# A decoder layer on one core: the causal mask of the first attention by GpSimd's selects instead of TensorE's mask matmuls, with new instruction orders and PSUM banks for the loop

## The reference

```python
q, k, v = split(x @ qkv_w.T + qkv_b)            # 16 heads of 8
q, k = relu(q) + 1e-6, relu(k) + 1e-6
kv = cumsum(einsum('bhld,bhle->bhlde', k, v), axis=2)
num = einsum('bhld,bhlde->bhle', q, kv)          # token l sees the tokens up to l
den = maximum(einsum('bhld,bhld->bhl', q, cumsum(k, axis=2)), 1e-6)
x = layernorm(x + (num / den) @ out_w.T + out_b)
x = layernorm(x + window_attention(x, ctx, ctx) @ W_proj.T + b_proj)   # softmax, |distance| <= 64
x = layernorm(x + experts(x))    # top 1 of 8 experts, capacity 641, gelu, 512 hidden
```

## Time and profile before

| | |
|---|---|
| time, median of 3 runs | 474.26 us (473.88 to 474.88) |
| profiled execution, its own time | 473.45 us |
| span of its instructions | 471.7 us |
| mean granted clock | 0.962 |
| busy of the span: PE, PEld | 89%, 72% |
| DVE, ACT, POOL | 75%, 57%, 55% |
| stretch 100 to 300 us, busy of 200 us: PE | 196.3 us |
| the same, DVE, ACT, POOL | 175.7, 141.2, 123.2 us |

### The profile page before, as it was taken

The page is one execution under the profiler, slowest core; times in us unless marked ns, Lnnn a source line. Parts: engine busy times, 40 slices in busy tenths (PEclk is TensorE's granted clock), DMA queues, the critical chain, the costliest instruction groups (busy, mean ns, idle before and its releaser), DMA issues.

```text
span 471.7 us, 20960 instructions
## 1 busy us (share of the span) xinstructions
PE 422.2 (89%) x7850; PEld 337.8 (72%) x7850; DVE 351.5 (75%) x1670; ACT 268.1 (57%) x655; POOL 258.6 (55%) x374
## 2 busy tenths in 40 slices
PE   8889999999999999999999999998746699999950
PEld 7666777778777778777777777776535478887740
DVE  4466667888888888888888898887673277778750
ACT  4456667667767667777667777666532333345400
POOL 5422355655666655666655666654552046757753
PEclk9999999999999999999999999999975799999995
DMA  4800000110110110110100100000014223334000
GB/s 137 266 15 15 14 25 15 31 33 25 29 35 26 33 31 27 30 32 26 37 27 27 34 18 20 20 17 13 19 35 118 85 84 103 103 108 134 25 17 20
DMA packets 25719, 22.50 MB, mean 48 GB/s; under 512 B 3606, under 2 KB 21072, under 8 KB 25620
## 3 DMA queue, kind: packets, MB, share of 16 engines
q1 hardware_dynamic: 23284, 16.96, 12.3%
q0 software_dynamic: 2336, 4.20, 2.8%
HBM read 12.13 MB, written 9.58 MB: 46 GB/s over the span
## 4 chain that ended last, share of the span: by engine, by line
PE 65%; ACT 17%; issue 9%; DVE 3%; POOL 2%; DMA 2%; POOLq 0%; ACTq 0%; DVEq 0%; SPq 0%
PE banks L567 24%; PE banks L623 13%; PE banks L810 8%; ACT arena L836 7%; PE banks L575 7%; ACT arena L936 6%; ACT arena L835 4%; PE banks L560 4%; PE banks L787 3%; PE banks L635 1%; DMA expert_in<-x,sidx 1%; PE banks L536 1%; PE banks L720 1%; PE banks L807 1%; DMA EB<-expert_in 1%
## 5 line engine op out<-in xcount | busy, mean ns | idle before, releaser
L1080 DVE TENSOR_REDUCE mx<-banks 128x8 f32<-128x1024 f32 x64 | 77.9, 1219 | 21.1 <-PE banks L575 21.1
L440 POOL TENSOR_TENSOR rs<-ve,minus_half 128x1 f32<-128x1 f32 x32 | 18.3, 570 | 105.1 <-DVE ve L1047 105.1
L865 ACT ACTIVATE arena<-banks 128x1024 f32<-128x1024 f32 x64 | 62.0, 1021 | 15.0 <-PE banks L575 15.0
L835 ACT ACTIVATE arena<-banks,first_half 128x512 f32<-128x512 f32 x64 | 44.1, 689 | 46.4 <-PE banks L575 46.4
L623 PE MATMUL banks<-arena,V 128*32 128x128 f32 x2048 | 69.4, 276 | 0.1
L936 ACT ACTIVATE arena<-banks,b1T 128x321 f32<-128x321 f32 x64 | 33.8, 529 | 55.1 <-PE banks L787 54.4
L623 PEld LDWEIGHTS banks<-arena,V 128*32 128x32 f32 x2048 | 51.9, 109 | 9.6 <-issue 5.3
L502 POOL DMA_INDIRECT out_x<-ot,idx x40 | 40.5, 1012 | 24.5 <-DVE ot L1277 15.8
L471 POOL DMA_INDIRECT expert_in<-x,sidx x32 | 35.5, 1109 | 11.5 <-DVE x L1153 4.8
L567 PE MATMUL banks<-x1T,CE 32*128 32x128 f32 x1024 | 37.5, 282 | 4.5 <-ACT arena L836 0.6
L567 PE MATMUL banks<-QE,kT 32*128 32x128 f32 x1024 | 37.7, 282 | 3.4 <-DVE mx L1080 1.3
(11 more groups left out here) (175 smaller groups left out, 1025.4 us busy)
## 6 DMA issues: line engine op xcount, KB each, us to landing
w_sb<-in_L_ffn_W SPq DMA_DIRECT2D x16, 256.0 KB, 3.1
expert_in<-zeros SPq DMA_DIRECT2D x10, 266.5 KB, 3.6
EB<-expert_in SPq DMA_DIRECT2D x8, 325.0 KB, 4.2
X<-in_x SPq DMA_DIRECT2D x32, 64.0 KB, 2.0
C<-in_ctx SPq DMA_DIRECT2D x32, 64.0 KB, 2.7
out_x<-fb SPq DMA_DIRECT2D x32, 64.0 KB, 1.5
out_x<-ot,idx POOLq DMA_INDIRECT x40, 2.2
b2b<-in_L_ffn_b SPq DMA_DIRECT2D x1, 512.0 KB
```

The source lines that it names most:

```text
L835: nc.scalar.activation(to[:, :, :, 0:W2C], at_bank[:, :, :, 0:W2C], ACT.Relu, scale=first_half[:])
L865: nc.scalar.activation(P2[b % 2][:, 2 * half:2 * half + 2].rearrange("p j a t -> p j (a t)"), pair("s2t", half), ACT.Exp, scale=SCALE).the ...
L1080: v.tensor_reduce(mx[b % 2][:, 8 * half:8 * half + 8].rearrange("p (j a) -> p j a", a=NA), pair("s2", half).rearrange("p j (a t) -> p j a ...
```

## The change

The 8 mask matmuls of `op_s1` go, and so do ACT's half-width copies: ACT now copies each half of the scores with one 128x1024 instruction. A new pair of POOL operations, `op_sel0` and `op_sel1`, sets to zero, in place in A1, the pairs that are not allowed, and `op_pv1` waits for them (`causal`) instead of for ACT. The copies of xT and x1T move from DVE to ACT. The order lists of all four engines and the bank table are new. The lags of several entries change with the place in the list at which a pass is cut.

```diff
+JOBS = [("xT", 0, (5,)), ("x2T", 8, (3,)), ("y2T", 6, (2,)), ("pv2", 4, (4,)), ("s1", 1, (6, 7, 2, 3)),
...
+            def keep_earlier(b, half):
+
+                pool.wait_ge(s1_out[half], b + 1)
+                part = A1[b % 2][:, 2 * half:2 * half + 2].rearrange("p j a t -> p (j a) t")
+                g.affine_select(out=part, in_=part, compare_op=ALU.is_ge, fill=0.0, base=0,
+                                pattern=[[0, 2 * NA], [1, P]], channel_multiplier=-1).then_inc(causal[half], 1)
...
-                by_head("s1", lambda part, a: kT[b % 2][part, :], lambda part, a: QE[b % 2][part, a, :])
-                causal_masks(0)
-                causal_masks(1).then_inc(s1_full, 1)
+                mm = by_head("s1", lambda part, a: kT[b % 2][part, :], lambda part, a: QE[b % 2][part, a, :], alone=True)
+                mm.then_inc(s1_full, 1)
...
-                values("pv1", b, A1[b % 2], V1[b % 2], s1_out).then_inc(pv1_full, 1)
+                values("pv1", b, A1[b % 2], V1[b % 2], causal).then_inc(pv1_full, 1)
...
-                nc.scalar.activation(to[:, :, :, 0:W2C], at_bank[:, :, :, 0:W2C], ACT.Relu, scale=first_half[:])
-                nc.scalar.activation(to[:, :, :, W2C:P], at_bank[:, :, :, W2C:P], ACT.Relu).then_inc(s1_out[half], 1)
+                nc.scalar.activation(A1[b % 2][:, 2 * half:2 * half + 2].rearrange("p j a t -> p j (a t)"),
+                                     pair("s1", half), ACT.Relu).then_inc(s1_out[half], 1)
```

More of the change, by code:

```diff
@@ L257, in decoder @@
         s1_out = [sem(f"s1_out{k}") for k in range(2)]
+        causal = [sem(f"causal{k}") for k in range(2)]
         pv1_full, yx1_done, t1_full, y1_ready = sem("pv1_full"), sem("yx1_done"), sem("t1_full"), sem("y1_ready")
@@ L475, in _ @@
             for n in range(B + LAST):
-                at(op_x1b, n - 3)
[L477 to L483, removed]
+                at(op_pow2, n - 6)
+                at(op_v2, n - 2)
+                at(op_QE, n)
+                at(op_x2, n - 6)
+                at(op_xb, n)
+                at(op_x1b, n - 3)
+                at(op_sel0, n)
+                at(op_pow1, n - 1)
+                at(op_sel1, n)
+                at(op_x1, n - 1)
                 at(op_scatter, n - 8)
@@ L535, in busy @@
                 for _ in range(count):
-                    pe.matmul(banks[:, 7, 0:P], ident[:], ident[:], start=True, stop=True)
+                    pe.matmul(banks[:, 4, 0:P], ident[:], ident[:], start=True, stop=True)
             busy(6)
@@ L560, in turned, with by_head @@
                 return pe.transpose(bank(name)[0:rows, 0:P], src, ident[:])
-            def by_head(name, weights, moved, first=True):
+            def by_head(name, weights, moved, first=True, alone=False):
                 for a in range(NA):
@@ L566, in by_head @@
                         part = slice(VW * j, VW * (j + 1))
-                        pe.matmul(banks[:, used, a * P:(a + 1) * P], weights(part, a), moved(part, a),
-                                  start=first and a == 0, stop=False, tile_position=(VW * j, 0))
+                        mm = pe.matmul(banks[:, used, a * P:(a + 1) * P], weights(part, a), moved(part, a),
+                                       start=alone or first and a == 0, stop=alone, tile_position=(VW * j, 0))
+                return mm
             lo, hi = slice(0, W2C), slice(W2C, P)
@@ L576, in masked @@
                                  tile_position=(at_rows.start, rows.start))
[L578 to L583, removed]
             def window_masks(name, half):
@@ L732, in _ @@
                     pe.wait_ge(setup_done, 1)
+                at(op_x2T, n - 8)
+                at(op_y2T, n - 6)
+                at(op_pv2, n - 4)
+                at(op_s1, n - 1)
+                at(op_y1T, n - 2)
+                at(op_lg, n - 8)
                 at(op_o2, n - 6)
@@ L828, in copied, with op_xTe @@
                 nc.scalar.copy(dst[:], bank(name)[:, 0:P]).then_inc(done, 1)
+            def op_xTe(b):
+                act.wait_ge(xT_full, b + 1)
+                wait(act, qkv_full, b - 1)
+                copied(xT[b % 2], "xT", xT_done)
             def op_s1e(b, half):
@@ L847, in op_yx1, with op_x1Te @@
                 nc.scalar.copy(yx1[:].rearrange("p j t -> p (j t)"), bank("pv1")[:, 0:2 * P]).then_inc(yx1_done, 1)
+            def op_x1Te(b):
+                act.wait_ge(x1T_full, b + 1)
+                wait(act, s2t_full, b - 1)
+                copied(x1T[b % 2], "x1T", x1T_done)
             def op_CE(b):
@@ L915, in _ @@
             for n in range(B + LAST):
+                at(op_x2Te, n - 8)
+                at(op_y2Te, n - 6)
+                at(op_yx2, n - 4)
+                at(op_xTe, n)
                 at(op_s1e0, n - 1)
@@ L1199, in _ @@
                     other_constants()
+                at(op_rec2, n - 4)
+                at(op_n2, n - 4)
+                at(op_den1, n - 1)
+                at(op_rk1, n - 8)
+                at(op_rec1, n - 1)
                 at(op_rk2, n - 8)
+                at(op_n1, n - 1)
+                at(op_fbs, n - 6)
                 at(op_rk3, n - 8)
-                at(op_rk4, n - 8)
-                at(op_fbs, n - 6)
-                at(op_mx0, n - 2)
-                at(op_den1, n - 1)
-                at(op_rec1, n - 1)
-                at(op_n1, n - 1)
-                at(op_mx1, n - 2)
+                at(op_mx0, n - 2)
+                at(op_mx1, n - 2)
+                at(op_mxh, n - 2)
+                at(op_y1Te, n - 1)
+                at(op_mxs, n - 2)
+                at(op_lg1, n - 7)
+                at(op_rk4, n - 8)
+                at(op_res2, n - 5)
+                at(op_res1, n - 1)
+                at(op_st1, n - 1)
+                at(op_mv1, n - 1)
             def rows_turned(e):
```

64 lines of the change are left out of this document (18 added, 46 removed), and 6 rows, old and new, of the table JOBS.

## The result

| | before | after |
|---|---|---|
| median of 4 runs | 474.57 us (473.88 to 475.54) | 539.71 us (535.54 to 541.78) |
| ratio, 95% interval | | 1.135 (1.129 to 1.142) |
| profiled execution, its own time | 473.45 us | 535.54 us |
| span | 471.7 us | 533.8 us |
| mean granted clock | 0.962 | 0.934 |

The kernel is slower, as forecast, but by 65 us and not by 21.6. The forecast of 496 and its range up to 508 are wrong.

What follows compares the result with a forecast made beforehand. A closed round (s1, ACT, s2t, pv1, s2, first maximum) of 10.07 us, PE nearly full, was taken as the bound; 473.45 + 21.6 (23 x 0.94, held slot) + 0.5 = 495.6, so 496 as median, range 475 to 508.

Steps and rivals of the forecast that it cites:

- The price of a select: On POOL, one 128x1024 fp32 select was put at 1.11 us, between bounds of 0.64 and 2.1.
- POOL's queue: POOL running selects, x1, scatter, pow2, V copy and QE from 2.42 to 9.36 us behind s1, with hardly a gap.
- The round with nothing held: Rival: slot passes ahead of QE, PE and ACT set a pass of 10.12 us; 474 to 478 us, chance 0.15.
- The experts and the drain: Parts outside the steady loop: experts not touched, the drain's chain as before but cut at another place; 0 us.
- the fill: First two sequences pay ACT, select and pv1 one after the other, uncovered: about 0.5 to 2 us.
- slot is held to QE's end at 9.36: DVE's slot held by POOL's QE, first maximum at 9.42; +0.94 us a pass in passes 9 to 31; chance 0.47.
- the layout: The new round's start times on all engines, counted from s1 = 0: first maximum at 9.42, next s1 at 11.01 us.
- The rival with fbs held: DVE's fbs itself held to 9.36 by the V copy and QE, 23 x 1.3 = 30 us; about 504, chance 0.22.
- slot is 0.15 long while QE runs: A sign in the new profile that would refute the forecast, which expected slot of about 1 us, ending with QE.
- 0.37 from maximum to s1: What PE needs between the end of the first maximum and s1: 0.37 us, kept for the new round.
- the change pays: Rival: yx1 and x1T's copy do not stop PE ahead of s2; 31 x -0.3 = -10 us, 464, chance 0.10.

Runs made afterwards that it cites:

- rk_fbs_behind: The changed kernel with DVE's op_fbs, op_rk2 and op_rk3 moved from ahead of the first maximum to behind the second; 482.3 us, ratio 1.013.
- rk_behind: The changed kernel with only DVE's op_rk2 and op_rk3 moved from ahead of the first maximum to behind the second; 507.02 us, ratio 1.068.
- orders_alone: The changed kernel's orders, banks and ACT copies of xT and x1T, but with PE's mask matmuls and half-width copies as before, no selects; 517.6 us, ratio 1.093.
- rc_psum: The changed kernel in its own orders, with rc, one of rcoh's two inputs, in PSUM instead of SBUF; 520.12 us, ratio 1.095.
- selects_alone: The kernel before, in its own orders and banks, with POOL's selects instead of PE's masks and full-width ACT copies; 470.52 us, ratio 0.992.
- gap_memset: rk_behind with a write-only POOL memset of 128x128 between the V copy and QE; 509.43 us, ratio 1.073.
- swap_QE_x2: selects_alone with QE ahead of x2 in POOL's list instead of behind it; 470.65 us, ratio 0.991.
- x2_ahead: rk_behind with POOL's x2 moved from behind QE to between pow2 and the V copy; 483.79 us, ratio 1.019.

## Why the prediction was wrong

**Right.** The direction and its kind: a DVE instruction with two SBUF inputs, held by POOL in front of the first maximum, in 22 sequences where 23 passes were said. The price of a select: 1.11 predicted, 1.10 measured. POOL's queue to 0.14. The round with nothing held: 10.12 was worked out, 10.11 measured (rk_fbs_behind), but this is partly luck: its first maximum starts 8.75 behind s1 (231.85 - 223.10), not 8.53, and s1 follows the end of the maximum after 0.14, not 0.37; the two errors cancel. The experts and the drain at 0 (1.5 measured), the fill at 0.5 to 2 (2.8 measured, a little more).

**The step that failed: "slot is held to QE's end at 9.36".** Two parts of it are wrong.

*Which instruction meets POOL.* I took slot as the first with two SBUF inputs that meets POOL's run, with fbs as the rival. The order shown ahead of the prediction has `rcoh<-rc,oh` two entries in front of fbs and five in front of slot, with two inputs from SBUF. The prediction has no term for it and does not ask what POOL does at that moment. It comes 7.67 behind s1, 0.43 into pow2, whereas before the change it took 0.15, beside x2 (at 231.88, x2 from 231.75 to 232.55). The hold starts 0.8 earlier than the 8.45 that the layout gave slot (8.2 and 0.25). And more stands behind it: between the end of `rcoh` and the first maximum DVE still runs `y`, fbs, rsum, over, slot and valid, 0.82 (235.65 to 236.47), where the layout had 0.06 for valid. `y` also brings the second wait on PE (1.15 ahead of pv2), with no counterpart in the sum.

*When a hold ends.* From the earlier trace rows, where a single POOL instruction stands by itself, I took the hold to be that of the instruction that it starts beside, or of QE. In the run of four it lasts from the arrival to the end of x2: 235.65 against the 234.83 at which QE ends, 0.8 more. So the hold ends at 10.04 behind s1 where the layout had 9.36, 0.68 later, and the work behind it takes 0.76 more: the first maximum starts at 10.86 instead of 9.42.

Set in the sum: a pass of 12.17 at full clock less 10.11 without a hold (a pass of rk_fbs_behind, where its clock is 1.00) is 2.06, times 23, 47 us, where 23 x (0.94 - 0.05) = 20.5 stood. The rival with fbs held had QE's end in it as well, which is why the range ended at 508. "The prediction is wrong if slot is 0.15 long while QE runs" was a poor test: slot never meets QE, it comes at 236.11. There it is held too, for 0.2, to the end of x1b on POOL (236.01 + 0.45 = 236.46, slot until 236.48).

**A term that was missing: the clock.** With PE's new waits (0.79 and 1.15 a pass) the granted clock is 0.87 in nine of the 23 passes: 23 x 0.41 = 9.4 us. The sum held PE idle 1 us a pass and left its pace as it was. With the hold gone (rk_fbs_behind) no passes at 0.87 stand in the steady loop, and none with a wait of 1.12 ahead of s1 (rk_behind) or of 0.8 (orders_alone). In rc_psum waits of about 0.5 and 1.6 ahead of s1 alternate, and most passes behind a wait of 1.6 are at 0.86 (12.08 instead of 11.75), though not the last ones. So the low clock goes with the longest waits; what decides it for a single pass is open, and no run fills these waits in the steady loop.

**A term mis-sized: 0.37 from maximum to s1.** It holds for the old orders and banks and was carried over to the new ones. Before the change s1 starts 0.36 to 0.41 behind the end of the first maximum in every pass that has one, whether PE idled 1.27 for it or 0.04; in selects_alone, with the same orders and banks, it is 0.36 again from the second of these passes on. In the changed kernel it is 0.10 to 0.14, and 0.10 in the pass shown (the maximum ends at 237.68, s1 starts at 237.78), and the same in orders_alone, so the selects are not what changed it. What makes up the difference was not taken apart. The resulting 0.27 went the other way and hid a part of the error.

**Together:** 0.04 for the new round, 2.06 for the hold, 0.41 for the clock are 2.51 a pass, 57.8 in 23 passes; fill 2.8 and tail 1.5 make the 62.1 of the span.

**The rival "the change pays"** (464, 0.10) had the gain of the mask right in kind: selects_alone shows it in the old order, 474.77 - 470.52 = 4.2 us. Its condition, that yx1 and x1T do not stop PE ahead of s2, did not hold in the new order.

## What to carry to other kernels

For each DVE instruction with two SBUF inputs, look in the timeline at what GpSimd runs when it starts, not only for the one under suspicion: the first in the queue that meets a GpSimd run takes the hold, and everything behind it inherits the delay; clearing one hands it to the next. Put such instructions behind the work that another engine waits for, or one of their inputs in PSUM. And before a new order is judged, run it without the edit that it comes with: here the edit was worth -4 us in the old order and the new order +43 without the edit (518 against 475). Together they cost 65, so the two do not add up: the selects make the run longer that DVE is held over.

## What the runs showed of the hardware

**A hold spans several GpSimd instructions.** It lasted 2.0 to 2.4 us over the V copy, QE and x2, in the changed kernel over the last 0.3 of pow2 as well, the longest of which takes 1.03. A memset among them did not end it. In the changed kernel, rk_behind and gap_memset it is there in 22 sequences each, from pass 10 to pass 31.

**Where it ends is not settled.** When the DVE instruction starts within 0.07 of QE's start, it is let go at QE's end (before the change, where nothing follows at once, and swap_QE_x2, where x2 does). When it starts beside pow2, beside the V copy, or 0.70 into QE (orders_alone), it is let go at x2's end, over every border between. Two cases stand against a rule by the distance to QE: one fbs of rc_psum starts 0.01 ahead of QE (252.38), with the V copy still running, and is held for 1.85, to x2's end; and the first `rcoh` of the changed kernel (85.07, pass 8) starts 0.86 into QE and is let go at its end after 0.20, though x2 follows. In the passes from 10 on xb, a TENSOR_TENSOR with two inputs, follows x2 with hardly a gap (it starts at 235.60 in the changed kernel) and does not prolong it. In pass 9 the same POOL operations, at the same distances, do not hold over the borders (fbs 0.28 in rk_behind), and a hold that starts 0.23 into QE ends 0.26 behind it (fbs at 96.10 in the changed kernel, 1.06, QE until 96.90). So it is not the kinds and distances of the neighbours alone that decide. From pass 10 on x2 and fbs wait for semaphores that they do not wait for in pass 9 (`wait(pool, fb_ready, b - 3)` and others take effect from b = 4); whether this is the reason, none of these runs tells.

**Beside x2 both are found.** fbs takes 0.21 when it starts with x2 or just ahead of it (x2_ahead), and before the change `rcoh` took 0.15, starting 0.13 into it. But in one pass of rc_psum fbs starts 0.11 into x2, which here follows QE, and is held to its end:

```profile
312.95 0.79 POOL L478 TENSOR_SCALAR x<-r,mv,rs 128x128 f32<-128x128 f32 x1
313.06 0.69 DVE L1093 SCALAR_TENSOR_TENSOR fbs<-rs,ve 128x1 f32<-128x1 f32 x1
```

**A custom DVE instruction is held like the others,** and frees with one operand in PSUM (104 ns against 2338).
